# A DLRM tower on one core: one of ten one-hot embedding tables is gathered instead, 17 gathers per tile for 16

## The reference

```python
e = stack([tbl_t[ids[:, t]] for t in range(26)], axis=1)      # 2048 x 26 x 128
c = concatenate([dense[:, None, :], e], axis=1)               # 2048 x 27 x 128
inter = einsum('bfd,bgd->bfg', c, c)[:, iu, ju]               # 351 pairs, upper triangle
h = concatenate([dense, inter, dense], axis=1)                # 2048 x 607
h = maximum(h @ W_top1 + b_top1, 0)                           # 512
h = maximum(h @ W_top2 + b_top2, 0)                           # 256
y = h @ W_top3                                                # 2048 x 1
```

## Time and profile before

| | |
|---|---|
| median of three runs | 400.0 us (397.94 to 400.47) |
| the profiled execution's own time | 398.94 us |
| its span, first to last instruction | 397.1 us |
| granted TensorE clock, mean | 0.991 |
| TensorE matmuls busy | 371.9 us (94%) |
| TensorE weight loads busy | 345.0 us (87%) |
| VectorE busy | 272.7 us (69%) |
| GpSimd busy | 243.2 us (61%) |
| ScalarE busy | 147.2 us (37%) |

### The profile page before, as it was taken

How to read it: one execution, slowest core, us unless ns; L and a number is a source line. 1 busy time by engine, 2 the same in 40 slices (tenths; PEclk the granted TensorE clock), 3 DMA queues, 4 the chain that set the end, 5 groups by cost and what they waited for, 6 DMA issues and landing times.

```text
span 397.1 us, 10186 instructions
## 1 busy us (share of the span) xinstructions
PE 371.9 (94%) x4392; PEld 345.0 (87%) x4392; DVE 272.7 (69%) x365; ACT 147.2 (37%) x355; POOL 243.2 (61%) x264
## 2 busy tenths in 40 slices
PE   0886899979999999999999999999999999999998
PEld 0765799869998999999998999999998999989976
DVE  2999989797775957488674957578584867633141
ACT  3777133643333332342333332343323423334341
POOL 6636557776756667575756757565765767567100
PEclk9999699999999999999999999999999999999999
DMA  7998544422323322232233314232331313122100
GB/s 186 260 242 209 177 149 107 119 62 68 105 69 101 81 66 83 81 89 74 78 97 86 95 45 103 75 94 69 82 104 57 98 51 107 42 60 56 33 3 0
DMA packets 19775, 37.38 MB, mean 94 GB/s; under 512 B 5930, under 2 KB 8626, under 8 KB 19732
## 3 DMA queue, kind: packets, MB, share of 16 engines
q0 software_dynamic: 8192, 16.79, 16.6%
q1 hardware_dynamic: 5492, 9.85, 9.4%
q10 hardware_dynamic: 6048, 10.10, 8.5%
HBM read 36.71 MB, written 0.01 MB: 92 GB/s over the span
## 4 chain that ended last, share of the span: by engine, by line
PE 75%; DVE 16%; issue 4%; ACT 2%; DMA 1%; SPq 0%; DVEq 0%
PE psB L439 32%; PE psG L465 14%; DVE one_hot L738 9%; PE psB L514 9%; PE psB L521 7%; PE psB L423 7%; PE psB L508 3%; DVE tab_lo L749 2%; DVE ZH L568 2%; PE psB L526 2%; DMA ET<-tbl 1%; DVE Zp L793 1%; PE psB L493 1%; PE psB L476 1%; ACT psG L613 1%
## 5 line engine op out<-in xcount | busy, mean ns | idle before, releaser
L362 POOL DMA_INDIRECT E<-tbl,gidx x256 | 242.3, 947 | 125.9 <-issue 70.4
L738 DVE TENSOR_TENSOR one_hot<-oidx,psR 125x1024 fp32r<-125x1024 int32 (+1 forms) x176 | 200.5, 1169 | 45.0 <-PE psB L439 40.5
L439 PE MATMUL psB<-one_hot,tab_hi 125*128 125x256 f32 x672 | 119.7, 300 | 11.2 <-ACT tab_hi L609 9.0
L439 PE MATMUL psB<-one_hot,tab_lo 125*128 125x256 f32 x672 | 112.4, 289 | 6.6 <-DVE tab_lo L749 3.5
L439 PEld LDWEIGHTS psB<-one_hot,tab_hi 125*128 125x128 f32 x672 | 94.5, 195 | 14.7 <-issue 9.5
L439 PEld LDWEIGHTS psB<-one_hot,tab_lo 125*128 125x128 f32 x672 | 95.2, 196 | 8.3 <-DVE tab_lo L749 5.0
L465 PE MATMUL psG<-ET 128*52 128x52 f32 x2048 | 62.2, 214 | 2.5 <-issue 1.2
L465 PEld LDWEIGHTS psG<-ET 128*52 128x52 f32 x2048 | 54.6, 128 | 10.8 <-issue 4.2
L641 ACT COPY ET<-psB 128x512 f32<-128x512 f32 x64 | 41.6, 649 | 35.9 <-PE psB L423 35.8
L670 ACT COPY S<-psG 116x208 f32<-116x208 f32 x64 | 21.3, 333 | 86.6 <-PE psG L465 84.9
L661 ACT COPY ET<-psB 128x256 f32<-128x256 f32 x80 | 27.4, 404 | 45.2 <-PE psB L439 45.2
(11 more groups left out here) (55 smaller groups left out, 213.1 us busy)
## 6 DMA issues: line engine op xcount, KB each, us to landing
oidx<-hot_idx ACTq DMA_DIRECT2D x35, 256.0 KB
E<-tbl,gidx POOLq DMA_INDIRECT x256
ET<-tbl SPq DMA_DIRECT2D x3, 448.0 KB
oidx<-hot_idx SPq DMA_DIRECT2D x5, 256.0 KB
dense<-dense_pairs SPq DMA_DIRECT2D x8, 128.0 KB
ZH<-tbl SPq DMA_DIRECT2D x2, 448.0 KB
S<-tbl SPq DMA_DIRECT2D x2, 448.0 KB
Zd<-dense_rows ACTq DMA_DIRECT2D x7, 128.0 KB, 2.0
```

Source lines behind the costliest of these rows:

```text
L362: nc.gpsimd.indirect_dma_start(E[:, n % SLOTS, i, :], None, gathered[feature_and_tile(n, i)[0]], bass.IndirectOffsetOnAxis(ap=gidx[:, 4 * ...
L439: product = nc.tensor.matmul(bank[:, t % 2 * DUO:(t % 2 + 1) * DUO], tab[0:ROWS_P, TABLE_BASE[t] + k0 + i, :], one_hot[0:ROWS_P, m % RING, ...
L738: nc.vector.tensor_tensor(one_hot[0:ROWS_P, m % RING, 0:many], ids, rows, ALU.is_equal).then_inc(hot_full[m % RING], 1)
```

## The change

One table of 1250 rows leaves the one-hot group and is gathered. `NS` becomes 9 and `NG` 17: 19 chunks per duo in place of 22, 17 gathers per tile in place of 16, 68 T groups in place of 64. As 17 is no multiple of 4, a T group can hold gathers of two tiles, and ACT then empties it by two copies; a cycle of four halves holds 17 groups (5, 4, 4 and 4). The tenth raw place and the gate on its load go. All numbers that derive from `NS` and `NG` move along: the split of table 8 stays at ("hot", 0, 13), `clear_G` comes at step 14, the first gather indices are 36 columns.

```diff
-HOT_TABLES = ((1000, 8), (1250, 2))
+HOT_TABLES = ((1000, 8), (1250, 1))
...
         raw_places = [(raw_ET, 0), (raw_ET, 1), (raw_ET, 2), (ZH, 0), (ZH, 1),
-                      (raw_S, 0), (raw_S, 1), (raw_w2, 0), (raw_S[:, 2 * TABLE_K[0] * D:], 0), (raw_ET, 0)]
-
+                      (raw_S, 0), (raw_S, 1), (raw_w2, 0), (raw_S[:, 2 * TABLE_K[0] * D:], 0)]
 
         VIA_PSUM = sum(k * D <= 2 * 512 for k in TABLE_K)
-        REUSED = NS - 1
...
                 rows = small[h].rearrange("(p k) d -> p (k d)", k=TABLE_K[h])
-                if h == REUSED:
-                    sp.wait_ge(raw_ready, 2)
```

## The result

The changed kernel takes 385.43 us (median of four runs, 383.07 to 385.88) against 400.11: a ratio of 0.9636, 95% interval 0.9613 to 0.966. Timed once more, for experiment 2, it was 387.58 against 399.72, 0.9688 (0.9639 to 0.9737). The profiled execution took 385.73 us, its span 383.8. The forecast was 381 us for the median, from a sum of 380.5 for the profiled execution. The kernel is faster and inside the range of 375 to 389; against the sum, the profiled execution lacks 5.2 us of the forecast gain.

The account below looks back on a forecast made before the run. TensorE was taken as the bound, GpSimd a close second limit. Steady part -15.5 and head -2.9 gave -18.4 on the profiled 398.9, 380.5 us; against the median 381.6, forecast 381, range 375 to 389.

Parts of the forecast that it names:

- The bound: Steady part: TensorE's full queue loses 20 matmuls, 2.38 us, in each of seven duos, 16.7 us; T groups add 1.2: -15.5.
- 13.1 were summed: Half 3 to the end: the share of the steady part's -15.5 us falling there, -13.1.
- It still fits, by 0.9 us: GpSimd in each duo: 34 gathers of 1.248 us need 42.4 of 43.3 us, so TensorE waits for none: 0.
- The last group's margin was to be 2.4: End of the kernel: the last gather group, T67, is ready 2.4 us before TensorE needs it; before, 2.8.
- the landing of 2.4: Gather groups: data taken as ready 2.4 us after the last gather's start; up to 5.2 not excluded.
- T21: Gather group in half 4, second run of five: given the least margin, 1.4 us; 0.6 with a landing of 3.2.
- not 10: GpSimd's waits for TensorE's transposes: only some 10 us in all, 6 of them before its fourth group.
- The head, -2.9: Duo 0: without 20 matmuls the first dot product comes at 46.4 in place of 49.34, -2.9 us.
- Here DVE sets the time: Head: VectorE's one-hots and table subtractions set the pace; the last subtraction ends 0.27 us later, TensorE's 3.1 us wait remains.
- 640 KB less in a head where the queues are full may help, and I count it at nothing: Head's table loads: one table less to load might help; counted as 0.
- 0, at worst +0.5 per duo: Pair step in steady duos: VectorE's copies to `U` come no later relative to TensorE: 0, at worst 3.5 us in all.
- The weights' load about 3 us earlier, which nobody waits for: SP's load queue: without table 9's load and wait, the weights' load starts about 3 us earlier, with no gain counted.

Follow-up runs that it names:

- experiment 2: The changed kernel, unchanged, profiled and timed once more: 387.58 us against 399.72, ratio 0.9688.
- experiment 6: Eight one-hot tables and 18 gathers per tile, on the changed kernel with its five weight steps moved to half 1, one chunk earlier still: 394.03 us, 0.9852.
- experiment 5: The changed kernel with the weight steps spread, three in half 1 and two in half 2: 381.46 us, 0.9536.
- experiment 12: The changed kernel with spread weight steps, four slots in E and the second and later gather groups held until the third table is cast: 381.61 us, 0.9546.
- experiment 3: The changed kernel with the five weight steps in half 1 in place of half 2: 381.32 us, 0.9559.
- experiment 1: The kernel before, unchanged, profiled once more, a single run: 399.81 us.

## Why the prediction was right, and what it missed

- **The bound.** TensorE's queue set the steady part: each duo lost what its 20 matmuls cost. From half 3 on 14.2 us went where 13.1 were summed; the 1.1 more was no term of the sum, so that it brought the total nearer is luck.
- **GpSimd, the second limit.** "It still fits, by 0.9 us", and TensorE waited for no gather. The last group's margin was to be 2.4; the last gather began at 356.62, with the landing of 2.4 it was there at 359.0, and its T group started at 360.81: 1.8. The landing of 2.4 was mostly too short: the waits of experiment 6 show 2.5 to 4.1, T21 in experiment 5 had 3.26, and only one wait, in experiment 12, shows less (2.2). In the changed kernel T21 itself had 3.0 by the same count, because TensorE came late to it, and the least margin was T11's, 1.4, which the prediction does not name. So that no gather was late owes something to the 6 us which TensorE lost before half 3. GpSimd's waits for L419 came to 15.6 us, not 10, 8.7 of them before the fourth group, because the first transposes came at 25.64 and not at 23.0. Experiment 5 took away TensorE's delay and the wait came at T21, as ranked; experiment 6 passed the limit.
- **The head, -2.9.** The step itself measured -2.8 (13.4 us from the last 1000-row subtraction to half 1, 16.2 before). What failed is "Here DVE sets the time" together with the term "640 KB less in a head where the queues are full may help, and I count it at nothing": the loads came slower, not faster, and VectorE waited for them. Its last 1000-row subtraction came 3.1 us later in this trace and some 1.7 on average. Why the loads are slower is open.
- **Half 2: the step that failed.** The prediction weighed VectorE's share of the pair step for a steady duo ("0, at worst +0.5 per duo") and never looked at half 2, the one half where the weight steps stand on ACT and VectorE too. There TensorE already waited 3.1 us in the kernel before (0.67, 0.33, 1.25 and 0.88 in front of L439, L476, L423 and L490). A chunk fewer between the weight steps and the pair transposes shortened the cover and not the chain. TensorE's waits grew to 4.6 us (0.30, 0.32, 1.89 and 2.08), by 1.5, and the 3.0 us at the low clock behind them cost about 1.4 more, an estimate from the same matmuls of the kernel before: together nearly the 3.1 lost. Experiments 2, 3 and 5 show it: the excess repeats, and most of it goes with the steps.
- **"The weights' load about 3 us earlier, which nobody waits for"** was nothing: the load was issued at 44.04, where it had been issued at 44.12, because the subtraction before it was late.

## What to carry to other kernels

When work leaves a full engine, sum each stretch by itself, above all those that occur once: where another engine's chain already made the full one wait, the removed work was cover, and the wait grows by it. Count the second engine's pitch from start to start, with its spare time group by group; here 17 gathers per tile fitted by 2% and 18 did not, and when TensorE reached half 3 some 5 us sooner, one group came late in a trace whose gathers had started late too, and with a fourth slot none did. A wait of TensorE can cost more than itself: behind those of 2 us in half 2 the matmuls ran for 3.0 us or more at a granted clock of 0.50. It need not: behind waits of up to 2.8 us in experiment 6, from 84 us on, the clock stayed at 1.00.

## What I had not expected of the hardware

Gathers that begin while VectorE subtracts with both inputs in SBUF are longer. The gather of 43.22 took 1.61 us under the subtraction of 42.52 to 44.01, like that of 40.05 before, and in the steady part this pair repeats:

```profile
87.13 0.43 DVE L786 TENSOR_TENSOR Zd_lo<-Zd,Zd_hi 128x256 fp32r<-128x256 f32 x1 [0.56 <-ACT Zd_hi L674]
87.28 1.10 POOL L360 DMA_INDIRECT E<-tbl,gidx  x1 [0.30 <-issue]
```

In this trace all six gathers over 1.0 us after the first one of the program, 1.02 to 1.61, began inside such an instruction; those that had begun 0.2 us ahead of one took 0.95. All six end 0.82 to 0.83 us after the subtraction does (43.22 + 1.61 = 44.83 against 44.01; 87.28 + 1.10 = 88.38 against 87.56), and so does the gather of 40.05 before. The rows fit a gather that is held until VectorE is done, and not one that is slowed in proportion. The Trainium skill, "SBUF — State Buffer", section "Who interferes with whom", says that a VectorE instruction with two SBUF inputs contends with a GpSimd instruction that reads SBUF. A gather reads its indices, `gidx`, from SBUF, and the rows agree: 1.02 to 1.61 us against 0.95.

Second, the DMA engines, at the same busy share of 1.05, moved 228 GB/s from 12 to 20 us in the changed kernel and 260 in the kernel before, though both load the same nine tables first. Unchanged and profiled again (experiments 1 and 2) they moved 241 and 251.
